# Eight more row maxima of the next row among the experts, 24 instead of 32 in the softmax units

## The reference

```
xn  = layernorm(x)
s   = attention_1(xn)          # 16 heads of 8, causal; weights 1 - tanh(energy)^2, normalised
h   = rmsnorm(xn) * norm1_w
q, k, v = h @ wq, h @ wk, h @ wv
X   = xn + softmax(q k^T / sqrt(8)) v @ wo          # 16 heads, no mask
h2  = rmsnorm(X) * norm2_w
combine = softmax of the two largest of softmax(h2 @ router_w), at their experts
moe = swiglu(h2, shared) + sum over 8 experts of combine_e * swiglu(h2, expert e)
out = x + s * silu(X + moe)
```

## Time and profile before

| | |
|---|---|
| median of 3 runs | 1154.11 us |
| profiled execution | 1157.05 us, span of its instructions 1155.2 us |
| TensorE (PE) busy | 1032.3 us, 89% |
| VectorE (DVE) busy | 856.3 us, 74% |
| ScalarE (ACT) busy | 652.9 us, 57% |
| GpSimd (POOL) busy | 347.4 us, 30% |
| reductions of line 677 | 512, mean 685 ns |
| mean granted TensorE clock | 0.970 of full speed |

### The profile page before, as it was taken

One profiled execution on the slowest core, in us unless ns is written; L12 is line 12 of the kernel. 1 busy time (PEld: TensorE's weight loads), 2 busy tenths in 40 slices (PEclk: granted clock), 3 DMA queues, 4 the chain that ended last, 5 costly groups with the idle time before them and its releaser, 6 DMA issues.

```text
span 1155.2 us, 18598 instructions
## 1 busy us (share of the span) xinstructions
PE 1032.3 (89%) x6912; PEld 471.8 (41%) x6912; DVE 856.3 (74%) x1716; ACT 652.9 (57%) x888; POOL 347.4 (30%) x194
## 2 busy tenths in 40 slices
PE   3459999989999999999999899999999889999998
PEld 1102355324652346423554245522465235542364
DVE  7447687759977597786877589775986869774872
ACT  4027862588326972378624884269723786248831
POOL 6500335103630154303352035400552033520023
PEclk9558999999999999999999999999999999999999
DMA  5540225103441045201251024310342113500020
GB/s 176 117 54 2 49 68 132 34 2 77 109 68 29 3 96 127 38 20 44 64 141 25 11 63 122 69 28 2 96 116 41 30 29 69 148 9 20 1 75 9
DMA packets 71785, 69.65 MB, mean 60 GB/s; under 512 B 8528, under 2 KB 63056, under 8 KB 71568
## 3 DMA queue, kind: packets, MB, share of 16 engines
q1 hardware_dynamic: 68928, 64.41, 24.7%
q10 hardware_dynamic: 2768, 4.06, 1.0%
HBM read 53.37 MB, written 14.81 MB: 59 GB/s over the span
## 4 chain that ended last, share of the span: by engine, by line
PE 56%; DVE 21%; ACT 11%; DMA 4%; issue 3%; SPq 3%; POOL 1%; ACTq 0%; DVEq 0%; POOLq 0%
PE O L1019 9%; PE O L1035 8%; DVE nmax L677 7%; DVE PT L714 7%; ACT PT L554 6%; PE S L1051 6%; PE S L1053 5%; PE S L994 5%; PE S L1052 5%; PE M L963 4%; PE M L960 4%; PE M L946 2%; DVE PT L840 2%; SPq L337 2%; SPq L327 1%
## 5 line engine op out<-in xcount | busy, mean ns | idle before, releaser
L554 ACT ACTIVATE PT<-S 128x1024 f32<-128x1024 f32 (+1 forms) x448 | 420.7, 971 | 117.3 <-PE S L994 115.0
L677 DVE TENSOR_REDUCE nmax<-M 128x1 f32<-128x512 f32 x512 | 330.6, 685 | 119.4 <-PE M L960 80.4
L714 DVE SCALAR_TENSOR_TENSOR PT<-PT 128x768 f32<-128x768 f32 (+1 forms) x192 | 215.6, 1171 | 96.4 <-ACT PT L554 96.0
L1019 PE MATMUL O<-PT,V 128*12 128x256 f32 (+3 forms) x2816 | 242.2, 424 | 0.0
L423 POOL TENSOR_TENSOR split<-split,parts 128x512 f32<-128x512 f32 x32 | 91.0, 2844 | 433.2 <-ACT parts L514 433.2
L438 POOL TENSOR_TENSOR PT<-PT,CB 128x1024 f32<-128x1024 f32 x56 | 133.2, 2385 | 278.0 <-DMA CB<-scrC 158.2
L588 ACT ACTIVATE PT<-S 128x1024 f32<-128x1024 f32 x72 | 73.9, 1027 | 250.7 <-PE S L1053 250.6
L994 PE MATMUL S<-stackQ,stackK 64*128 64x512 bf16 (+3 forms) x1024 | 192.1, 347 | 21.6 <-DMA stackQ<-mTZ 8.4
L1051 PE MATMUL S<-h2hi,wgu_hi 128*128 128x512 f32 x288 | 150.5, 522 | 0.1
L1035 PE MATMUL O<-PT,wdn 128*128 128x512 f32 x288 | 142.7, 595 | 0.0
L960 PE MATMUL M<-KX,stackQ 128*128 128x512 bf16 x256 | 104.3, 409 | 28.5 <-DMA KX<-scrK 21.3
(11 more groups left out here) (189 smaller groups left out, 1042.5 us busy)
## 6 DMA issues: line engine op xcount, KB each, us to landing
CB<-scrC SPq DMA_DIRECT2D x64, 256.0 KB, 5.7
stackQ<-scrQ SPq DMA_DIRECT2D x192, 64.0 KB
stackK<-scrK SPq DMA_DIRECT2D x192, 64.0 KB
scrQ<-parts SPq DMA_DIRECT2D x16, 384.0 KB, 5.0
scrK<-parts SPq DMA_DIRECT2D x16, 384.0 KB, 7.8
KX<-scrK SPq DMA_DIRECT2D x96, 32.0 KB
PT<-in_w_gu ACTq DMA_DIRECT2D x2, 1152.0 KB, 8.0
xin<-in_x SPq DMA_DIRECT2D x8, 256.0 KB, 2.9
```

Of the source, the lines that this page charges most:

```text
L554: a.activation(PT[:, n % SLOTS, 2 * q * w:2 * q * w + 2 * w].rearrange("p (r n) -> p r n", r=2), S[k][:, :].rearrange("p (r n) -> p r n", ...
L677: v.tensor_reduce(nmax[:, h % 2, h // 2, t:t + 1], M[k][:, :], AX.X, ALU.max, negate=True).then_inc(m_read[k], 1)
L714: v.scalar_tensor_tensor(p, p, 1.0, p, ALU.subtract, ALU.mult).then_inc(weighed, 1)
L1019: last = t_.matmul(O[k][32 * q:32 * q + VW, i0:i1], V[:, j, 4 * g + q, :], PT[:, n % SLOTS, w * q + at:w * q + at + i1 - i0], start=(j == ...
```

## The change

The first eight maxima of Y (heads 8 and 9), called EARLY, move from units 0 to 4 of their own row to experts 7 and 8 of the row before, and with it: KX holds five head pairs, EARLY uses KX, the first pass makes them for row 0. The table is laid out anew: X begins at expert 1 instead of 2, W at expert 4 instead of 5; the Y and Z maxima left in units 0 to 8 are 2, 3, 3 and 3, 3, 3, 3, 2, 2 (before 1, 3, 4, 4, 4 and 3, 4, 4, 5). The parts of Y follow unit 2 instead of 4, maxT_Y stands at unit 4 instead of 5. In units 2 to 8 this makes 19 maxima instead of 28, since unit 0's and unit 1's are 2 and 3 now instead of 1 and 3.

```diff
-PADDED = 4
+PADDED = 5
@@
-spread(MAX["Y"], {0: 1, 1: 3, 2: 4, 3: 4, 4: 4})
-spread(MAX["Z"], {5: 3, 6: 4, 7: 4, 8: 5})
-PLACES[3].insert(2, "outT")
-PLACES[5].insert(2, "maxT_Y")
+EARLY = MAX["Y"][:8]
+spread(MAX["Y"][8:], {0: 2, 1: 3, 2: 3})
+spread(MAX["Z"], {3: 3, 4: 3, 5: 3, 6: 3, 7: 2, 8: 2})
+PLACES[3].insert(1, "outT")
+PLACES[4].insert(1, "maxT_Y")
@@
-spread(MAX["X"], {EXPERT + e: n for e, n in enumerate((0, 0, 5, 4, 4, 3))})
-spread(MAX["W"], {EXPERT + 5 + e: n for e, n in enumerate((2, 6, 6, 2))})
+spread(MAX["X"], {EXPERT + e: n for e, n in enumerate((0, 3, 5, 5, 3))})
+spread(MAX["W"], {EXPERT + 4 + e: n for e, n in enumerate((2, 6, 6, 2))})
+spread(EARLY, {EXPERT + 7 + e: n for e, n in enumerate((4, 4))})
@@ VectorE, row
-                    if n == 4:
+                    if n == 2:
                         maxima_parts(u, "Y")
@@ VectorE, first pass
+            for name in EARLY:
+                maximum(FIRST, name)
@@ TensorE, maximum
-                if name in MAX["X"] or name in MAX["W"]:
+                if name in AHEAD:
```

More of the change, by code:

```diff
@@ L95 @@
 PLACES[END] += ["maxT_W", "outL"]
-AHEAD = {"xnT", "hT", "Q2", "K2", "V2", "Q1", "K1", "V1", "maxT_X", *MAX["X"], "maxT_W", *MAX["W"]}
+AHEAD = {"xnT", "hT", "Q2", "K2", "V2", "Q1", "K1", "V1", "maxT_X", *MAX["X"], "maxT_W", *MAX["W"], *EARLY}
 class Uses:
```

## The result

The changed kernel took 1176.58 us, median of 4 runs (1175.14 to 1178.78), against 1154.29 for the kernel before, median of 4: a ratio of 1.0202 with a 95% interval of 1.0170 to 1.0234. It is 22.3 us slower; the forecast was 10.7. The time lies inside the stated range of 1152 to 1180, but the change is twice the one forecast. Its profiled execution took 1176.66 (span 1174.9), which is 19.6 more than the profiled execution before. That one had been 2.9 above the median of its first three runs, as the prediction said.

What follows compares the result with a forecast made beforehand. VectorE was taken to pace the softmax part, TensorE the experts. 7 x 6.7 for experts, less 8 x 4.7 for softmax, plus 1.4 at the start, gave +10.7 us: 1167.8 profiled, 1164.8 against the median; range 1152 to 1180.

Steps and rivals of the forecast that it cites:

- the price of the softmax part: Softmax units 2 to 9: fewer maxima give back 4.7 us a row, bounds 3.0 and 6.7.
- one that stands directly ahead of a pair costs TensorE next to nothing: Softmax units: a maximum directly ahead of a score pair is almost free; one behind a pair was priced at 0.32 us.
- no longer late: Softmax part: VectorE's own sum, 22 reductions by 0.62 and 1.8 of other work, is 15.4 us against TensorE's 15.6.
- the 2.1 of unit 6: Softmax units 5 and 6: each takes 2 x 0.87 + 0.32 = 2.1 us.
- Rival 4: Softmax part gives only its lower bound, 3.0 us a row: +24, 1178; chance 0.13.
- (a): Experts: eight more KX products cost 1.8 us, one more maximum in unit 0's place 0.2; together 2.0 a row.
- (b): Expert 1: six names bring three waits, expert 2 starts 4.1 us later, 3.4 a row of it waiting.
- (c): Expert 3: seven names and a GpSimd hold of VectorE's line 700 make TensorE wait 1.2 us a row.
- The rule of the Trainium skill that the prediction named: GpSimd reading SBUF first fully blocks VectorE's two-SBUF-input instructions and two-port casts; expert 3's term would be 1.6.
- Rival 3: Expert 3: GpSimd holds line 700 for a whole 2.39 us instruction; a row pays 7.3: +14.9, 1169; chance 0.20.
- (d): Experts 5 and 6: expert 5's seventh name costs 0.5 us, an X-parts wait of 0.8 becomes 0.4; sum 0.1.
- The start: First pass: 98 KB more of KX transfers cost +1.4 us, or +5 if its eight maxima are not hidden.

Runs made afterwards that it cites:

- experiment 2: Changed kernel with each maximum left in the softmax units multiplying 256 columns instead of 512: 1162.60 us, ratio 1.0077 to the kernel before.
- Experiment 1: Softmax half of the change alone: experts as in the kernel before, maxima of heads 8 and 9 set to zero once, not computed: 1131.12 us, ratio 0.9799.
- experiment 3: Kernel before with its X maxima spread 3, 5, 4, 3, 1 from expert 1 on, none added, softmax units untouched: 1176.69 us, ratio 1.0210.
- experiment 4: Changed kernel with VectorE at expert 1 taking four names ahead of its up product instead of two: 1152.77 us, ratio 1.0012 to the kernel before.
- 5: Changed kernel with eight unread 512-column products ahead of the second X maximum of expert 1: 1175.00 us, ratio 1.0179 to the kernel before.
- experiment 7: Kernel before with KX of five head pairs instead of four and nothing else: 1158.45 us, ratio 1.0028.
- Experiment 9: Half the move against the kernel before: EARLY is four maxima, all at expert 8, X and W left in place: 1143.43 us, ratio 0.9911.

## Why the prediction came out as it did

**The step that failed is the price of the softmax part, 4.7 a row where 3.4 was measured; over eight rows that is 10.4 us.** Two sentences of it were wrong. The first is "one that stands directly ahead of a pair costs TensorE next to nothing". It was read from two starts 0.01 apart. A start says when an instruction enters the array, not what it takes away from the next. The pair uses all 128 rows of the array, and whichever half the maximum holds, one of the two scores stands behind it. The durations in the same group would have said so; it costs 0.22, and experiment 2 shows that it does. The second is that VectorE is "no longer late": on the sum it isn't (14.48 of 17.8 us), but with two buffers TensorE still stood 0.57 for it in unit 2 and 0.56 in unit 6, and the 2.1 of unit 6 had no wait in it.

Counted by units: 5 took 2.26 (forecast 2.1), 6 took 2.69 (2.1), 7 and 8 took 2.17 and 2.18 (1.94, which was ScalarE's bound and not reached), 2 to 4 together 8.48 (8.0). That is 1.7 over the forecast's own units, of which it had allowed 0.4 by taking 4.7 (16.5 us) and not the 16.1 of its list. In units 5, 7 and 8 it is 0.6, and the maxima ahead of pairs; in unit 6 it is 0.6, and the wait; in units 2 to 4 it is 0.5, with both in it, and no run separates them. Experiment 1 shows the amount; experiment 2 shows the first cause. That the wait of unit 6 costs its full 0.56 is read from the timeline and not from a run without it. Rival 4, with 3.0 a row and 1178, was nearest, and by its reason: maxima that still cost TensorE their time, and two buffers that stumble.

The Trainium skill, page "TensorEngine Tiling (Array Packing)", section "Theoretical Speedup", gives a small dimension of up to 64 a speedup of up to twice. The two scores of a pair agree with it (0.39 for both records together, as long as one product of 128 rows). A maximum ahead of a pair doesn't get it: it is a third such product for two halves, and paid the full 0.22. A second maximum behind the same pair, the fourth product, does get it (510.90).

**(a) and (b) held.** The eight products cost 1.84 by their places (0.23 each), and the ninth, in unit 0, nothing: from unit 0 to unit 2 it is 7.63 us in both kernels. The second KX product went 1.96 after step 3's last product and the third 1.09 later (1.8 and 1.1 forecast). combT waited 0.23 and not 0.4, and expert 1 grew by 3.83 against 4.1, 3.15 of it waits against 3.4. Experiment 3 shows these waits as a cost by themselves, 4 takes them away.

**(c) held in the rows without a dip:** 1.66 in experts 3 and 4, less two products, is 1.2, the value taken. The rule of the Trainium skill that the prediction named is seen at work (315.99). Rival 3 had the right cause, but the hold was 1.4 long and not the whole 2.39, and the price stayed at 1.2. In the rows with a dip it was 0.4.

**What was missing: the clock.** Nothing in the prediction asked what TensorE does after it has stood. Net it is 0.8 in four of seven rows, 3 us in all, by the rows' lengths. It stands only behind the waits, but not behind all of them (experiments 2 and 5), and what decides is open.

**(d):** 0.26 instead of 0.1 in experts 5 and 6, with 0.37 at both places; the 0.63 ahead of maxT_X went. **The start** (+1.4) is not seen at the first row of this profile and is 3.2 (0.9 to 5.5) by experiment 7.

**The sum,** against the profiled forecast of 1167.8: softmax part +10.4, experts +1.8 (7 by 0.25, nearly all of it the clock), start -1.4, the two longer rows of before that didn't come again -2.0, behind the last row -0.3: +8.5. Measured +8.9. The other 2.9 between forecast and median is the profile of before, which lay above its median, while that of the changed kernel doesn't.

Experiment 9 with the number of experiment 4 in addition was not tried, nor a third buffer.

## What to carry to other kernels

Price a product by how far apart its neighbours start with it and without it, never by when it starts; a record of its neighbour that is longer behind it is the same message. When work is moved off a late engine, find the point at which another sets the pace: here half of the move paid and the other half did not. An engine that isn't late on the sum of a stretch can still hold another up inside it. And where two engines share a ring of two buffers, follow the order in which the reader empties them: reading two names ahead of one long instruction was worth 24 us.

## What the runs showed of the hardware that I had not expected

- TensorE's clock fell behind a stretch with 2.5 us of waiting in 3.1: granted 0.54 of full speed over 3.7 us at 586.20, products of 512 columns 0.43 us apart instead of 0.23. It did so in four of seven rows in the changed kernel and in four in experiment 3, in none of seven in experiment 2 behind the same waits, and in none when eight products filled 1.90 of them. The same wait on TensorE can bring the dip in one row and not in the next.
- The dip partly pays for itself: it moves VectorE's line 702 past most of a GpSimd instruction that otherwise holds it for 1.4 us.
- Three products of 48, 64 and 64 rows, started within 0.01 us, take 0.22 longer than the two of 64 alone, and 0.11 longer when the first has 256 columns. A fourth, of 48 rows, started 0.23 behind them, adds nothing (0.53 to the V step with three and with four).
